# A sequence layer in which eight of 32 key tiles are summed from half-precision parts made by VectorE, with the two halves of the sums stored and loaded apart

## What is computed

```python
q, k = l2norm(split16(ln(x) @ w_q)), l2norm(split16(ln(x) @ w_k))   # 16 heads of 16
v = split16(x @ w_v)
resonance = 0.5 + 0.5 * tanh((q @ k.T - 0.27) * 15.0)
modulation = resonance * gate_q[..., :, None] * gate_k[..., None, :]
fused = modulation @ v
x = layernorm(x + fused @ w_o + b_o)
h = silu(fp4(x) @ fp4(w_gate).T) * (fp4(x) @ fp4(w_up).T)
x = layernorm(x + fp4(h) @ fp4(w_down).T)
```

## Time and profile before

| | us |
|---|---|
| median of 3 runs (4379.05 to 4384.3) | 4383.23 |
| profiled execution | 4378.88 |
| its span | 4377.1 |
| TensorE busy in it | 4111.8 (94%) |
| ScalarE busy | 4017.1 (92%) |
| VectorE busy | 1561.6 (36%) |
| GpSimd busy | 159.5 (4%) |

### The profile page before, as it was taken

The page is one execution under the profiler, slowest core; times in us unless marked ns, Lnnn a source line. Parts: engine busy times, 40 slices in busy tenths (PEclk is TensorE's granted clock), DMA queues, the critical chain, the costliest instruction groups (busy, mean ns, idle before and its releaser), DMA issues.

```text
span 4377.1 us, 69385 instructions
## 1 busy us (share of the span) xinstructions
PE 4111.8 (94%) x28776; PEld 1285.9 (29%) x28776; DVE 1561.6 (36%) x4540; ACT 4017.1 (92%) x3271; POOL 159.5 (4%) x120
## 2 busy tenths in 40 slices
PE   7988899999999999999999999999999999999997
PEld 5651222222222222222222222222222222222223
DVE  6754023333333332333233333333333333333236
ACT  4669999999999999999999999999999999999993
POOL 2330000000000000000000000000000000000001
PEclk9999999999999999999999999999999999999998
DMA  4454444344434443444334433443345334433450
GB/s 114 124 129 78 70 76 65 61 68 78 65 63 67 78 68 60 66 78 71 60 63 78 77 55 62 78 78 56 61 78 78 56 61 78 78 59 59 77 83 13
DMA packets 179871, 313.70 MB, mean 72 GB/s; under 512 B 65264, under 2 KB 141808, under 8 KB 154608
## 3 DMA queue, kind: packets, MB, share of 16 engines
q1 hardware_dynamic: 179568, 309.41, 42.1%
HBM read 266.82 MB, written 42.47 MB: 71 GB/s over the span
## 4 chain that ended last, share of the span: by engine, by line
PE 69%; ACT 23%; DVE 4%; issue 3%; DMA 1%; SPq 1%; POOL 0%; POOLq 0%; DVEq 0%; ACTq 0%
PE ps L1268 35%; ACT room L706 22%; PE ps L1258 20%; PE ps L1295 8%; PE ps L1318 4%; DMA m_f<-fused_t 1%; DVE room L858 1%; PE ps L1213 0%; DVE st L812 0%; DVE xnT L848 0%; PE ps L1224 0%; PE ps L1308 0%; DVE sm L773 0%; DVE sm L774 0%; DVE sm L775 0%
## 5 line engine op out<-in xcount | busy, mean ns | idle before, releaser
L706 ACT ACTIVATE room<-ps 128x1024 f32<-128x1024 f32 (+1 forms) x2816 | 3787.1, 1417 | 178.4 <-PE ps L1258 162.2
L1268 PE MATMUL ps<-room,vt 128*32 128x512 f32 x16384 | 2051.2, 601 | 0.0
L1258 PE MATMUL ps<-qs,room 64*128 64x512 f16 x8198 | 1325.9, 383 | 203.7 <-ACT room L706 182.6
L1258 PEld LDWEIGHTS ps<-qs,room 64*128 64x128 f16 x8198 | 310.4, 93 | 1749.5 <-ACT room L706 1123.1
L1268 PEld LDWEIGHTS ps<-room,vt 128*32 128x32 f32 x16384 | 388.1, 108 | 945.3 <-issue 945.3
L1295 PE MATMUL ps<-wguT,m_xqT 128*128 128x352 f32 x960 | 348.2, 485 | 0.0
L967 DVE TENSOR_TENSOR vz<-ps,vz 128x352 f32<-128x352 f32 x120 | 63.0, 525 | 757.7 <-ACT vz L716 757.7
L972 DVE TENSOR_TENSOR vz<-ps,vz 128x352 f32<-128x352 f32 x120 | 63.0, 525 | 595.9 <-PE ps L1295 595.9
L1318 PE MATMUL ps<-wdnT,wqk 128*128 128x256 f32 x720 | 198.9, 404 | 0.6 <-DVE wqk L937 0.6
L1295 PEld LDWEIGHTS ps<-wguT,m_xqT 128*128 128x128 f32 x960 | 162.6, 189 | 105.2 <-issue 54.3
L600 POOL TENSOR_TENSOR m_x<-m_x,bo 128x256 f32<-128x256 f32 x60 | 43.9, 731 | 3876.7 <-DMA m_x<-in_L_attn_x_dram 3876.7
(11 more groups left out here) (172 smaller groups left out, 2198.0 us busy)
## 6 DMA issues: line engine op xcount, KB each, us to landing
room<-k_parts SPq DMA_DIRECT2D x520, 256.0 KB, 9.4
vt<-v_gated SPq DMA_DIRECT2D x65, 1024.0 KB, 17.9
qs<-q_parts SPq DMA_DIRECT2D x520, 32.0 KB, 10.1
gqb<-q_gates SPq DMA_DIRECT2D x256, 64.0 KB, 2.2
room<-in_L_attn_x_dram SPq DMA_DIRECT2D x16, 512.0 KB, 4.1
v_gated<-vz SPq DMA_DIRECT2D x64, 128.0 KB, 2.2
fused_t<-fs SPq DMA_DIRECT2D x256, 32.0 KB, 1.7
q_parts<-room SPq DMA_DIRECT2D x30, 256.0 KB, 2.4
```

Source lines behind the costliest of these rows:

```text
L706: act.activation(res[:, c, o:o + m, :], ps[:, o:o + m, :], ACT.Sigmoid, scale=2 * SHARP / QK_UP ** 2, bias=-2 * SHARP * THRESH).then_inc(b ...
L1258: ins = pe.matmul(ps[:, BANK[n % 2] + i, :], ks[o:o + HROWS, par, h // 2, kt * P:(kt + 1) * P], qs[o:o + HROWS, par, h // 2, :], start=Tru ...
L1268: ins = pe.matmul(ps[32 * h:32 * h + 32, SUM_BANK, :], vt[:, par, n * HD:n * HD + 32], r, start=kt == 0, stop=kt == KT - 1, skip_group_che ...
```

## The change

Of the 32 key tiles, eight (0, 3, 6, 12, 15, 18, 21, 24: `SPLIT` times three) are no longer summed in fp32 in the units from 4 on. VectorE turns their sigmoids, 2048 columns, into a half-precision high part and a half-precision rest (`split_results`, two operations), and TensorE multiplies both parts with values that hold their own high part and rest in 32 columns per head (`split_sums`, eight fp16 matmuls). Such a tile is summed behind group 4c + 4 where it stood behind 4c. The bank's rows 0 to 15 of a head then hold the sums with the high values, rows 16 to 31 those with the rests. `store_sums` stores both halves, eight transfers, `load_sums` loads them apart, and GpSimd adds them (`m_f` plus `m_f2`). In the tail TensorE adds them by multiplying both.

The values are scaled by a power of two drawn from the largest value: VectorE keeps running maxima in the projection phase, a turn and a broadcast on TensorE find the largest at its end (`largest_value`, `value_scales`), and `scale_values` scales `vt` for the next unit and makes the parts of its eight tiles, ahead of `end_unit`, which takes the scale back out. The first tile summed is now 1 (`FIRST_KT`), from a padded copy `vp`, which needs one more load. VectorE's work on the token tiles is written in another order, with a `split_results` between its steps. SP issues the query gates behind the loads of `x` and of the sums.

```diff
+def split_at(n):
+
+    return [SPLIT.index(c) for c in SPLIT if 4 * c + 4 == n]
...
+SPLIT = [0, 1, 2, 4, 5, 6, 7, 8]
...
-                    sp.dma_start(fd[b, (g * HG + h) * HD:(g * HG + h + 1) * HD, bass.ds(i * BLK, BLK)],
-                                 fs[32 * h:32 * h + HD, :]).then_inc(b_st, 16)
-
-            def load_sums(dst, j, t):
+                    for lo in range(2):
+                        o = 32 * h + lo * HD
+                        sp.dma_start(fd[b, lo, (g * HG + h) * HD:(g * HG + h + 1) * HD, bass.ds(i * BLK, BLK)],
+                                     fs[o:o + HD, :]).then_inc(b_st, 16)
+
+            def load_sums(hi, lo, j, t, done):
 
                 b, i = j // QB, j % QB
-                return sp.dma_start(dst, fd[b, :, bass.ds(i * BLK + t * P, P)].rearrange("(c r) t -> r c t", r=P))
+                for m, dst in enumerate((hi, lo)):
+                    sp.dma_start(dst, fd[b, m, :, bass.ds(i * BLK + t * P, P)].rearrange("(c r) t -> r c t", r=P))\
+                      .then_inc(done, 16)
 
...
-                for h in range(HG):
-                    sp.dma_start(gqb[32 * h:32 * h + 32, :],
-                                 gqd[b, g * HG + h:g * HG + h + 1, bass.ds(i * BLK, BLK)]
-                                 .to_broadcast([32, BLK])).then_inc(b_gq, 16)
                 if begins(j, g):
                     k = u - HG
                     wait(sp, l_r, k)
                     sp.sem_inc(sp_pass, 1)
                     sp.dma_start(m_x[:, :], x_tile[k]).then_inc(l_x, 16)
 
-                    sp.wait_ge(b_st, 16 * HG * u)
+                    sp.wait_ge(b_st, 16 * NST * u)
                     sp.sem_inc(sp_pass, 1)
-                    load_sums(m_f[:, :, :], j - 1, g).then_inc(l_f, 16)
+                    load_sums(m_f[:, :, :], m_f2, j - 1, g, l_f)
+                for h in range(HG):
+                    sp.dma_start(gqb[32 * h:32 * h + 32, :],
+                                 gqd[b, g * HG + h:g * HG + h + 1, bass.ds(i * BLK, BLK)]
+                                 .to_broadcast([32, BLK])).then_inc(b_gq, 16)
...
+                    pool.wait_ge(l_f, 16 * NFL * (k + 1))
+                    pool.tensor_tensor(m_f[:, :, :], m_f[:, :, :], m_f2, ALU.add).then_inc(l_fs, 1)
...
+            def largest_value():
+
+                after(dve.tensor_reduce(v_mx, vmx[:, 0:TB], AX_X, ALU.max))
+                dve.tensor_scalar(v_mx, v_mx, 2.0 ** -100, None, ALU.max).then_inc(v_mxd, 1)
+                dve.wait_ge(v_row, 1)
+                after(dve.tensor_reduce(v_one, ps[0:1, C_BANK, 0:P], AX_X, ALU.max))
+                dve.tensor_scalar(v_one.bitcast(I32), v_one.bitcast(I32), EXPONENT, None, ALU.bitwise_and)\
+                   .then_inc(v_oned, 1)
+
...
+            def scale_values(u):
+
+                par, split = u % 2, u >= HG
+                dve.wait_ge(b_in[par], 16 * NIN * (u // 2 + 1))
+                wait(dve, v_pad, 1)
+                ins = dve.tensor_scalar(vp[:, par], vp[:, par], v_up, None, ALU.mult)
+                ins = dve.tensor_scalar(vt[:, par], vt[:, par], v_up, None, ALU.mult)
+                if not split:
+                    ins.then_inc(b_v, 1)
+                    return
+                after(ins)
+                v4 = vt[:, par].rearrange("p (k h d) -> p k h d", k=KT, h=HG)
+                parts = []
+                for i, n in ((0, 3), (3, 5)):
+                    k = 3 * SPLIT[i]
+                    two = vh[:, par, i:i + n].rearrange("p i (h m d) -> p i h m d", h=HG, m=2)
+                    parts.append((v4[:, k:k + 3 * n - 2:3], two[:, :, :, 0], two[:, :, :, 1]))
+                for v, hi, lo in parts:
+                    ins = dve.tensor_scalar(hi, v, 1 / RES_UP, None, ALU.mult)
+                after(ins)
+                for v, hi, lo in parts:
+                    ins = dve.scalar_tensor_tensor(out=lo, in0=v, scalar=1 / RES_UP, in1=hi,
+                                                   op0=ALU.mult, op1=ALU.subtract)
+                ins.then_inc(b_v, 1)
 
             def inverse_roots(k, par, n):
 
...
+                    after(dve.tensor_reduce(vmx[:, TB:2 * TB], vz[:, par, :, 0:D], AX_X, ALU.max,
+                                            apply_absolute_value=True))
+                    after(dve.tensor_tensor(vmx[:, 0:TB], vmx[:, 0:TB], vmx[:, TB:2 * TB], ALU.max))
+                    if isinstance(n, int) and n == NBLK - 1:
+                        largest_value()
...
+            def split_results(u, g, i):
+
+                n = 4 * SPLIT[i]
+                r = res[:, (NGRP // 2 * g + n // 2) % RES_CYCS, 0:HG, :].rearrange("p h n -> p (h n)")
+                if i >= 2:
+
+                    dve.wait_ge(b_pv, u * KT + SPLIT_POS[i - 2] + 1)
+                dve.wait_ge(b_act, u * NGRP + n + 1)
+                after(dve.tensor_scalar(r_hi[i % 2], r, RES_UP, None, ALU.mult))
+                dve.scalar_tensor_tensor(out=r_lo[i % 2], in0=r, scalar=RES_UP, in1=r_hi[i % 2],
+                                         op0=ALU.mult, op1=ALU.subtract).then_inc(b_cv, 1)
...
-                if ends(j, g):
-                    end_transposes(u - HG - 1)
                 if begins(j, g):
-                    begin_tile(u - HG, g % 2)
-                if ends(j, g):
-                    end_tile(u - HG - 1, (g - 1) % 2)
-                if begins(j, g):
-                    gates(u - HG)
+                    k, par = u - HG, g % 2
+                    if ends(j, g):
+                        end_transposes(k - 1, (0,))
+                    split_results(u, g, 0)
+                    if ends(j, g):
+                        end_transposes(k - 1, (1,))
+                    split_results(u, g, 1)
+                    begin_tile(k, par)
+                    split_results(u, g, 2)
+                    begin_quantize(k, par)
+                    if ends(j, g):
+                        end_tile(k - 1, 1 - par)
+                    split_results(u, g, 3)
+                    turned(k)
+                    split_results(u, g, 4)
+                    for p in range(4):
+                        gates(k, (p,))
+                        if p < 3:
+                            split_results(u, g, 5 + p)
+                    hidden(k)
                 if isinstance(j, int) and j == 0:
                     if g == 0:
...
+                if u + 1 < NUNIT:
+                    scale_values(u + 1)
                 end_unit(u)
...
+            def split_sums(i, par):
+
+                for part in (r_hi[i % 2], r_lo[i % 2]):
+                    for h in range(HG):
+                        ins = pe.matmul(ps[32 * h:32 * h + 32, SUM_BANK, :], vh[:, par, i, 32 * h:32 * h + 32],
+                                        part[:, h * BLK:(h + 1) * BLK], start=False, stop=False, skip_group_check=True)
+                ins.then_inc(b_pv, 1)
...
+                    split = not isinstance(j, int) or j >= 1
                     for kt in sums_at(n):
-                        if kt == 0:
+                        if kt == FIRST_KT:
                             pe.wait_ge(b_ev, u + 1)
-                        sums(kt, par, g)
+                            pe.wait_ge(b_v, u + 1)
+                        if not (split and is_split(kt)):
+                            sums(kt, par, g)
+                    for i in split_at(n):
+                        if split:
+                            pe.wait_ge(b_cv, (u - HG) * NSPLIT + i + 1)
+                            split_sums(i, par)
                     if n in END and ends(j, g):
```

More of the change, by code:

```diff
@@ L69, in sums_at, with is_split @@
             at[4 * c] = [3 * c - 1, 3 * c]
-        at[4 * c + 2] = [0, 1] if c == 0 else [3 * c + 1]
+        at[4 * c + 2] = [1, 0] if c == 0 else [3 * c + 1]
     return at.get(g, [])
+def split_at(n):
+    return [SPLIT.index(c) for c in SPLIT if 4 * c + 4 == n]
 assert sorted(k for g in range(NGRP) for k in sums_at(g)) == list(range(KT))
+SPLIT = [0, 1, 2, 4, 5, 6, 7, 8]
+NSPLIT = len(SPLIT)
+RES_UP = 2.0 ** 12
+V_TOP = 2.0 ** 22
+FIRST_KT = 1
+NST, NFL = 8, 2
+def is_split(kt):
+    return kt % 3 == 0 and kt // 3 in SPLIT
 FH = F // 2
+SPLIT_POS = []
+for g in range(NGRP):
+    for i in split_at(g):
+        SPLIT_POS.append(sum(not is_split(k) for n in range(g + 1) for k in sums_at(n)) + len(SPLIT_POS))
 BEGIN = {7: "P", 19: "X", 23: "G0", 27: "G1", 31: "G2", 35: "G3"}
@@ L93 @@
 FFN_LOADS = 5
-A_CHAIN = 14
+A_CHAIN = 16
 RING = 8
@@ L833, in inverse_roots @@
                 rsqrt(y, v, ha, tmp)
+                if isinstance(n, int) and n == NBLK - 1:
+                    value_scales()
+                    scale_values(0)
             def norm_x(k, par):
@@ L927, in to_grid, with end_transposes @@
                 return dve.tensor_tensor(dst.rearrange("p (n e) -> p n e", e=16), t3, bcast(scale, 16), ALU.mult)
-            def end_transposes(k):
-                for half in range(2):
+            def end_transposes(k, halves=(0, 1)):
+                for half in halves:
```

(6 more changed lines are left out.)

83 lines of the change are left out of this document (63 added, 20 removed).

## The result

The changed kernel takes **4474.06 us** (median of 4 runs, 4470.4 to 4478.96) beside 4383.72 of the kernel before, measured with it: a ratio of **1.0209, 95% interval 1.0191 to 1.0227**. It is slower, well clear of the noise, though the interval does not exclude a little less than 2%. The forecast was 4466. (One launch of a later experiment, the one with one half alone, took 5570.03 us at a granted clock of 0.63 and is left out of its figures.) The profiled execution took 4478.96 us, its span 4477.2; that of before took 4378.88.

The account below looks back on a forecast made before the run. TensorE was taken to set the periods with a feed-forward piece, ScalarE's 5.41 us being the floor elsewhere. 4378.9 + 57 for 60 units + 30 once only gave 4466 us (own bounds 4440 to 4500), range 4355 to 4545.

Parts of the forecast that it names:

- the two places: Where VectorE's added work delays TensorE each unit: last gate piece to next unit's first piece, 1.15 us; tile 12's parts, 0.9.
- Ceiling of the gain: TensorE's periods in a unit, if VectorE never came late: 61.4 us after against 62.3 before, at most 0.9 saved.
- Part pairs: VectorE's conversion and subtraction over 2048 columns: 1.23 and 2.28 us, 3.57 a pair with gaps, 28.6 a unit.
- rival of a slow conversion: VectorE's conversion runs at one column a cycle, each pair 4.64 us, parts late at three groups: 4601 us; chance 0.10.
- Value scaling: VectorE's added scaling passes before the unit's end: 3.9 us, with 2.28 for the pass over 2048 columns.
- GpSimd held off by VectorE: Rival: GpSimd's sum of the halves starts only when VectorE's subtraction ends, 0.5 us later: 4493 us; chance 0.13.
- the rival at 4406: Value scaling at the fast rate, or transfers landing a microsecond sooner: P on time, tile 12 still late; chance 0.17.
- Delay of P: The next unit's first piece on TensorE, after scaling, stores, loads and GpSimd's sum, comes 1.15 us late each unit.
- Tile 12: VectorE normalizes the previous token tile before splitting tile 12, so TensorE waits 0.9 us for its parts at group 20.
- Projection phase: Added reduction and maximum in VectorE's statistics chain lengthen each block by 1.4 us, 21 in all, once only.
- Boundary and tail: Last maximum, broadcast and first scaling before first scores: +6 us; extra stores and loads in the tail: +3.
- The rival that VectorE is never late: Only the 0.9 us a unit gain counts: 4357 us, or 4340 with the projection phase's additions hidden; chance 0.15.

Follow-up runs that it names:

- the one with one half alone: Changed kernel without storing, loading or adding the second halves of the sums: 4422.24 us, 1.0088 of the kernel before.
- the three moves: Changed kernel with running maxima after the next block's normalization, GpSimd's halves before its bias, token-tile normalization after the fourth part pair: 4372.76 us, 0.9978 of the kernel before.
- the last experiment: On top of the three moves, sums from tile 6's parts taken at group 16 instead of group 12: 4351.99 us, 0.9926 of the kernel before.

## Why the prediction was right, and where it was not

The sign, the size and the two places were right: 4466 forecast, 4474 measured, and of the 100.1 us between the profiled executions every stretch but one within 5 us.

**Ceiling of the gain: the right size, somewhat too high.** The periods were added up to 61.4 us, a gain of 0.9 a unit. The unit of the three moves shown above, in which VectorE is never late, takes 61.78: a gain of 0.54. Part of the difference stands in the sum itself. It calls 5.41 the floor that ScalarE sets and then puts 5.19 for period 16; that period takes 5.40, with TensorE waiting 1.08 in it for ScalarE. Only with one set of parts placed otherwise do the units come to 61.67, with 0.32 of waiting left before P.

**Part pairs: right.** 1.23 and 2.28 were taken, 1.22 and 2.29 measured (2.31 on average for the one tensor where GpSimd's addition sometimes begins first). The rival of a slow conversion falls.

**Value scaling: wrong in size.** The step read a rate from one row: 0.414 us at 256 columns with two per-partition scalars. One row at one size cannot tell a slope from a start. The rows of after can: one such scalar costs 1279 ns at 2048 columns where the constant form L1110 takes 1218, and at 128 columns 280, where the constant form's start and slope give 0.22. So, as an estimate from these rows, each such scalar adds some 0.06 to the start and leaves the rate alone; two at 256 columns make 0.29 + 0.12 = 0.41, the row that misled. (The Trainium skill, "VectorE: DVE Perf Modes", The perf-mode tier table, gives 1227 ns for fp32 `tensor_scalar` at 2048 columns; the trace agrees within 5%, with 1279.) The whole scaling took 2.97 and not 3.93, and `fs` is held up by 0.2 us at most.

**GpSimd held off by VectorE: a rival's mechanism, mostly at another instruction.** It had 0.13. With a value scaling about one us shorter P would have been nearly on time, as the rival at 4406 has it. Instead the bias addition, which stands ahead of the sum of the halves in GpSimd's order, fell into VectorE's subtraction in 51 of 60 units and took 2175 ns on average in place of 731. (The Trainium skill, "SBUF — State Buffer", Summary: rules for kernel authors: if a VectorE instruction has two SBUF inputs while the GpSimd one reads SBUF, the second to be issued is fully blocked until the first finishes. The trace agrees, in both orders: the addition that began at 2124.00, inside the subtraction, ended 0.6 after it, and where GpSimd began first the subtraction took 2.86 for 2.29.) The prediction looked for this at the sum of the halves, where it struck in eight units only; in the others it struck the instruction in front, which the prediction had not costed since it was there before. The two errors, in the unit shown about one us too much and 0.8 too little, nearly cancelled, and that was luck: P came 20.35 after the last gate product, 20.7 was forecast. The total was closer than its steps.

**Delay of P, per unit:** TensorE waits 0.71, and with the second halves left out the unit is 0.79 shorter; the forecast had 1.15, less the 0.22 that the period at 8 gives back. **Tile 12:** 0.73 of waiting, 0.70 a unit when it is removed, forecast 0.9. The sum of these measured terms, 62.32 + 0.79 + 0.70 - 0.54 = 63.27, is close to the measured unit of 63.20.

**Projection phase: the mechanism right, the term mis-sized.** 1.4 us a block were counted at unchanged clock, 21 in all; it was 36. At full clock a block is 1.6 longer, 24 in all, and the other 12 or so came with a granted clock at the lower level in part of the blocks, for which the prediction had no term. The experiment with the maxima moved gives back all of it, so both belong to that one placement. **Boundary and tail:** +7.0 and +3.3, forecast 6 and 3. No experiment was made on these.

**The rival that VectorE is never late** (4357, or 4340 with the projection phase's additions hidden) counts on the gain of 0.9 a unit. With the three moves, which take most of VectorE's waits away and hide these additions, it is 4373; the 4352 of the last experiment needs another placement of one set of sums besides, which that rival did not have.

**Slips in the sums.** The blocked sum is 0.5 a unit and 60 units make 30 where 27 is written, and the fast value pass takes 1.05 off the 0.95 and leaves -0.10, not -0.05, so 4403 for 4406. Neither moves the forecast or its range.

## What to carry to other kernels

An engine at a third of its time is no free room. The added work cost most of its time at three places where it stood ahead of something another engine was due for. When one instruction or short group was moved at each, two of these costs went away and the third was more than halved (the wait before P, 42.5 to 16.6 us in the kernel with the three moves); with one more move, and no work taken out, 4474 became 4352. So after an offload read, for each handover that passes through the newly loaded engine, how long before it was due it used to arrive. And cost the instructions that were already there as well: one of them took three times as long on average, because its neighbour on another engine had changed.
